# Adding the row term inside PSUM with a three-row bf16 matmul, and keeping the exponentials there

## What is computed

```
el, er = sum(z * attn_l), sum(z * attn_r)
e = leaky_relu(el[src] + er[dst], 0.2)
m = segment_max(e, dst)
ex = exp(e - m[dst])
denom = segment_sum(ex, dst)
out = segment_sum(ex / denom[dst] * z[src], dst) + z
```

## Time and profile before

| what | value |
|---|---|
| time, median of 2 runs | 3789.61 us |
| the two runs | 3783.88 and 3795.34 us |
| span of the profiled execution | 3780.9 us |
| TensorE matmul busy | 2914.6 us (77%) |
| VectorE busy | 1979.8 us (52%) |
| ScalarE busy | 1219.4 us (32%) |

### The profile page before, as it was taken

One profiled execution on the slowest core, in us unless ns is written; L12 is line 12 of the kernel. 1 busy time (PEld: TensorE's weight loads), 2 busy tenths in 40 slices (PEclk: granted clock), 3 DMA queues, 4 the chain that ended last, 5 costly groups with the idle time before them and its releaser, 6 DMA issues.

```text
span 3780.9 us, 46025 instructions
## 1 busy us (share of the span) xinstructions
PE 2914.6 (77%) x14456; PEld 2141.7 (57%) x14457; DVE 1979.8 (52%) x3392; ACT 1219.4 (32%) x1944; POOL 235.8 (6%) x267
## 2 busy tenths in 40 slices
PE   6874999978499996849369269649995994945995
PEld 4542888864288886425257124238884552534773
DVE  6745999945699984551431234556641434233113
ACT  1122778842277774230024101133320222001110
POOL 0000000000000000000001300000000000000112
PEclk9987999989799998979569679869997997965996
DMA  1011121121111212001335621122222100123435
GB/s 61 0 45 46 51 66 55 57 61 34 45 60 54 67 44 62 33 28 29 122 111 196 184 102 60 62 94 78 71 64 96 44 33 20 31 95 110 163 128 168
DMA packets 102475, 276.89 MB, mean 73 GB/s; under 512 B 25358, under 2 KB 38104, under 8 KB 99115
## 3 DMA queue, kind: packets, MB, share of 16 engines
q1 hardware_dynamic: 66794, 194.26, 14.1%
q0 software_dynamic: 32976, 73.59, 7.5%
q10 hardware_dynamic: 2600, 7.68, 0.5%
HBM read 204.99 MB, written 72.91 MB: 74 GB/s over the span
## 4 chain that ended last, share of the span: by engine, by line
PE 42%; DMA 13%; DVE 6%; issue 2%; ACT 1%; SPq 1%; POOL 1%; ACTq 0%; DVEq 0%; POOLq 0%
PE psum L914 16%; PE psum L870 12%; DMA arena<-raw 6%; PE psum L1032 4%; PE psum L1041 4%; PE psum L941 3%; DMA arena<-y_rows,arena 2%; PE psum L931 2%; DVE arena L1460 1%; DMA arena<-r_rows 1%; DMA arena<-xn_rows,arena 1%; PE psum L860 1%; DMA arena<-x 1%; DVE arena L1488 1%; DMA arena<-el_rows 1%
## 5 line engine op out<-in xcount | busy, mean ns | idle before, releaser
L914 PE MATMUL psum<-arena 125*125 125x256 f32 (+3 forms) x2400 | 626.1, 421 | 84.6 <-DVE arena L1490 84.6
L870 PE MATMUL psum<-arena 128*125 128x384 f32 (+1 forms) x1840 | 663.2, 520 | 0.0
L941 PEld LDWEIGHTS psum<-arena 125*125 125x125 f32 x4800 | 580.3, 191 | 71.7 <-DVE arena L1485 16.7
L914 PEld LDWEIGHTS psum<-arena 125*125 125x125 f32 x2400 | 449.5, 189 | 256.3 <-issue 66.9
L941 PE MATMUL psum<-arena 125*125 (+1 forms) x4800 | 568.3, 271 | 16.7 <-DVE arena L1485 16.6
L870 PEld LDWEIGHTS psum<-arena 128*125 128x125 f32 x1840 | 347.6, 191 | 291.2 <-issue 121.9
L1460 DVE CUSTOM_DVE_ANT_0 arena<-arena,no_edge_bias 125x1250 bf16<-125x1250 f32 x300 | 436.5, 1455 | 79.7 <-DMA arena<-el_rows 73.1
L931 PE MATMUL psum<-arena,spread 126*125 126x313 f32 (+1 forms) x1344 | 437.7, 449 | 33.4 <-DMA arena<-r_rows 18.7
L1485 DVE SCALAR_TENSOR_TENSOR arena<-arena,edge_counts 125x625 f32<-125x625 f32 x480 | 381.9, 805 | 79.5 <-ACT arena L1200 79.3
L1187 ACT ACTIVATE arena<-arena,el 125x625 f32<-125x625 f32 x480 | 386.4, 806 | 38.4 <-DMA arena<-el_rows 38.4
L1200 ACT ACTIVATE arena<-psum,el 125x625 f32<-125x625 f32 x336 | 262.6, 782 | 200.9 <-PE psum L931 179.2
(11 more groups left out here) (192 smaller groups left out, 2631.8 us busy)
## 6 DMA issues: line engine op xcount, KB each, us to landing
arena<-el_rows SPq DMA_DIRECT2D x54, 610.4 KB
arena<-in_L_ffn_W SPq DMA_DIRECT2D x16, 1152.0 KB, 9.1
y_rows<-arena SPq DMA_DIRECT2D x47, 384.0 KB, 2.4
arena<-raw SPq DMA_DIRECT2D x40, 375.0 KB
arena<-r_rows SPq DMA_DIRECT2D x24, 610.4 KB
arena<-in_L_w SPq DMA_DIRECT2D x16, 768.0 KB, 6.2
arena<-in_L_gnn_W SPq DMA_DIRECT2D x4, 3072.0 KB, 12.7
z_heads<-arena POOLq DMA_DIRECT2D x10, 1000.0 KB, 12.3
```

Of the source, the lines that this page charges most:

```text
L870: ins = e.matmul(bank[0:P, 0:w], L.xt[u][:, k, :], L.w_sb[:, k, at:at + w], start=(k == 0), stop=(k == L.KT - 1))
L914: ins = e.matmul(banks[2 + 2 * (j % 2) + c][0:P, 0:w], Ph[half][:, s, d * P:(d + 1) * P], (L.zh[u] if L.spill else L.z)[:, s, at:at + w], ...
L941: ins = e.matmul(banks[2 + half][0:P, d * 65:(d + 1) * 65], Ph[half][:, s, d * P:(d + 1) * P], L.z[:, s, h, :], start=(s == 0), stop=(s == ...
```

## The change

The VectorE additions go, and with them `ADD_AT`, the broadcast copies `rb2`, the matrix `spread` and the slots of `r2` and `L.ex`. The block now stays in its pair of PSUM banks from the first stage to the last:

1. `relu` writes straight to `block_exponents(j)` in PSUM. There are two such places, so relu of j may start only when weights of j - 2 are done, and it waits for that on `p_ready`. It is issued after exponentials of j - 2 (before: j - 3).
2. TensorE adds the row for all 20 blocks, in place: a matmul by `ones3` (three rows of ones, bf16) over three partitions that hold r cut into three bf16 parts, with `start=False`.
3. `exponentials` reads and writes the same place in PSUM.
4. `weights` reads it from PSUM.

`max_end`, which now also cuts r into three parts, has ten small VectorE instructions where it had five; the DRAM round trip carries three bf16 rows and takes one load where there were seven. Four matmuls per layer write banks 4 to 7 once before the first block (`primed`).

```
+            if L.batched:
+                    q = r_part[:, u * 3 * T:(u + 1) * 3 * T].rearrange("p (j t) -> p j t", j=3)
+                    st.add(e.scalar_tensor_tensor(out=v[0], in0=er, scalar=SLOPE, in1=v[1], op0=ALU.mult, op1=ALU.subtract))
+                    st.wait()
+                    st.add(e.tensor_copy(r_bf[:, 0:T], v[0]))
+                    st.wait()
+                    st.add(e.tensor_copy(q[:, 0, :], r_bf[:, 0:T]))
+                    st.add(e.tensor_tensor(v[1], v[0], r_bf[:, 0:T], ALU.subtract))
+                    st.wait()
+                    st.add(e.tensor_copy(r_bf[:, T:2 * T], v[1]))
+                    st.wait()
+                    st.add(e.tensor_copy(q[:, 1, :], r_bf[:, T:2 * T]))
+                    e.tensor_tensor(q[:, 2, :], v[1], r_bf[:, T:2 * T], ALU.subtract).then_inc(L.r_ready, 1)
...
-            def lay_r2(h, u, i, first, more):
+            def lay_r3(h, u, i):
                 e.wait_ge(L.rt_sb, L.since["rt_sb"] + h + 1)
                 apart(e)
+                e.dma_start(r3_rows[h, :, :], L.rt3[u]).then_inc(L.r_out[u], 16)
                 e.wait_ge(L.r_out[u], L.since["r_out"][u] + 16 * (i + 1))
                 apart(e)
                 if not isinstance(i, int) or i > 0:
+                    e.wait_ge(L.t_ready, L.since["t_ready"] + 2 * T * (h - 1))
                     apart(e)
+                e.dma_start(L.r3[u], r3_rows[h, :, :].rearrange("(j t) p -> j (t p)", j=3)).then_inc(L.r3_in[u], 16)
...
-                e.wait_ge(L.e_ready, L.since["e_ready"] + 2 * T * h + j + 1)
                 o = block_exponents(j)
                 for at, to in ((0, CUT), (CUT, HALF)):
-                    ins = e.matmul(o[:, at:to], spread[:, :], L.r2[half][:, s % 3, at:to], start=True, stop=True)
+                    ins = e.matmul(o[:, at:to], ones3[:, :], L.r3[u][:, half * HALF + at:half * HALF + to],
+                                   start=False, stop=True, skip_group_check=True)
                 ins.then_inc(L.t_ready, 1)
...
+                e.wait_ge(L.p_ready, L.since["p_ready"] + 2 * T * h + j + 3)
                 apart(e)
-                e.activation(L.r2[half][0:P, s % 3, :], L.erb[u][:, half * HALF:(half + 1) * HALF], ACT.Relu,
+                e.activation(block_exponents(j), L.erb[u][:, half * HALF:(half + 1) * HALF], ACT.Relu,
                              bias=L.el8[:, s, bass.ds(h, 1)], scale=1.0 - SLOPE).then_inc(L.relued, 1)
...
+                e.wait_ge(L.t_ready, L.since["t_ready"] + 2 * T * h + j + 1)
                 apart(e)
-                e.activation(L.ex[j % 4], src, ACT.Exp, bias=L.el2[:, s, bass.ds(h, 1)]).then_inc(L.e_ready, 1)
+                e.activation(block_exponents(j), block_exponents(j), ACT.Exp, bias=L.el2[:, s, bass.ds(h, 1)]).then_inc(L.e_ready, 1)
...
-                    if j + 3 < 2 * T:
-                        relu(h, u, i, j + 3)
+                    if j + 2 < 2 * T:
+                        relu(h, u, i, j + 2)
...
-                    e.scalar_tensor_tensor(out=Ph[half][:, s, :], in0=L.ex[j % 4], scalar=2.0, in1=counts,
+                    e.scalar_tensor_tensor(out=Ph[half][:, s, :], in0=block_exponents(j), scalar=2.0, in1=counts,
                                            op0=ALU.min, op1=ALU.mult).then_inc(L.p_ready, 1)
```

More of the change, by code:

```diff
@@ L38 @@
 BAL_EPS = 0.01
-ADD_AT = [3, 7, 9]
-ADDS, TURNS = 2 * len(ADD_AT), 2 * (T - len(ADD_AT))
-def of_vector(j):
-    return sum(v % T in ADD_AT for v in range(j))
 def split(total, parts):
@@ L253, in graph_transformer @@
         r_rows = dram("r_rows", (12, 2 * T, P))
+        r3_rows = dram("r3_rows", (12, 3 * T, P), BF16)
         z_heads = dram("z_heads", (4, N, 512))
@@ L342, in graph_transformer @@
                 at += 2 * N
-                L.r2 = [carve(at + half * 3 * HALF, P + 1, 3 * HALF).rearrange("p (u d) -> p u d", u=3) for half in range(2)]
-                at += 6 * HALF
+                L.r3 = [carve(at + u * HALF, 3, HALF).bitcast(BF16) for u in range(2)]
+                at += 2 * HALF
                 L.ex = [carve(at + u * HALF, P, HALF) for u in range(4)]
@@ L348, in graph_transformer @@
                 at += 4 * HALF
-                L.rb2 = [carve(at + u * N, P, N) for u in range(2)]
-                at += 2 * N
+                L.rt3 = [carve(at + u * 63, 3 * T, 63).bitcast(BF16)[:, 0:P] for u in range(2)]
+                at += 126
             else:
@@ L536, in lay_r2 @@
                 if not isinstance(i, int) or i > 0:
-                    e.wait_ge(L.added, L.since["added"] + ADDS * (h - 1))
+                    e.wait_ge(L.t_ready, L.since["t_ready"] + 2 * T * (h - 1))
                     apart(e)
-                e.dma_start(L.rb2[u], over(r_rows[h, T:2 * T, :].rearrange("t p -> (t p)"))).then_inc(L.rb2_in[u], 16)
-                for half in range(2):
-                    if not first:
-                        e.wait_ge(L.t_ready, L.since["t_ready"] + TURNS * (h - 1) + TURNS // 2 * (half + 1))
-                        apart(e)
-                    for v in range(3):
-                        e.dma_start(L.r2[half][P:P + 1, v, :],
-                                    r_rows[h, T + half * HT:T + (half + 1) * HT, :].rearrange("(o t) p -> o (t p)", o=1)
-                                    ).then_inc(L.r2_in[half], 16)
-                    if half == 0 and more:
-                        load_el(h + 2, u)
+                e.dma_start(L.r3[u], r3_rows[h, :, :].rearrange("(j t) p -> j (t p)", j=3)).then_inc(L.r3_in[u], 16)
             def move_r(h, u, i):
@@ L577, in rows_of @@
                     load_er(h, u)
-                    lay_r2(h, u, i, False, more)
+                    lay_r3(h, u, i)
+                    if more:
+                        load_el(h + 2, u)
                 with e.Fori(1, L.H // 2 - 1) as i:
@@ L945, in sum_tile, with batched_head @@
                     e.matmul(banks[1][0:1, 0:1], ident[:, 0:1], ident[:, 0:1], start=True, stop=True).then_inc(L.p_free, 1)
-            def batched_head(h, u, first, last):
+            def batched_head(h, u, i, first, last):
                 for j in range(2 * T):
                     half, s = j // T, j % T
-                    if s not in ADD_AT:
-                        exponents(h, j)
+                    exponents(h, u, i, j)
                     if not (first and half == 0):
@@ L955, in batched_head @@
                         turn_r(h + 1, 1 - u)
+            if L.batched:
+                for b in range(4, 8):
+                    ins = e.matmul(banks[b][0:P, 0:512], noti[:, :], MB[:, 0, 0:512], start=True, stop=True)
+                ins.then_inc(L.primed, 1)
             turn_r(0, 0)
             if L.batched:
-                batched_head(0, 0, True, False)
-                batched_head(1, 1, False, False)
+                batched_head(0, 0, 0, True, False)
+                batched_head(1, 1, 0, False, False)
                 with e.Fori(1, L.H // 2 - 1) as i:
                     for u in range(2):
-                        batched_head(2 * i + u, u, False, False)
-                batched_head(L.H - 2, 0, False, False)
-                batched_head(L.H - 1, 1, False, True)
+                        batched_head(2 * i + u, u, i, False, False)
+                batched_head(L.H - 2, 0, L.H // 2 - 1, False, False)
+                batched_head(L.H - 1, 1, L.H // 2 - 1, False, True)
                 for d in range(HT):
@@ L1313, in graph_vector @@
         def graph_vector(e, st):
[L1314 removed]
+            e.wait_ge(gs["in"], 16 * 5)
             st.add(e.memset(zero, 0.0))
+            st.add(e.memset(ones3[:, :], 1.0))
             for w in range(2):
@@ L1528, in finish @@
                     ins.then_inc(L.out_done, 1)
-            def add_r2(h, u, i, j):
-                half, s = j // T, j % T
-                if j == ADD_AT[0]:
-                    e.wait_ge(L.rb2_in[u], L.since["rb2_in"][u] + 16 * (i + 1))
-                e.wait_ge(L.relued, L.since["relued"] + 2 * T * h + j + 1)
-                e.wait_ge(L.p_ready, L.since["p_ready"] + 2 * T * h + j + 1)
-                apart(e)
-                e.tensor_tensor(L.ex[j % 4], L.r2[half][0:P, s % 3, :], L.rb2[u][:, half * HALF:(half + 1) * HALF], ALU.add).then_inc(L.added, 1)
             def batched_head(h, u, i, first, more):
```

59 lines of the change are left out of this document (27 added, 32 removed).

## The result

The changed kernel takes 4312.47 us (two runs, 4310.36 and 4314.57). The kernel before takes 3789.61. The ratio is 1.1376, interval 1.1339 to 1.1413: slower by 13.8%. The forecast of 4101 us had the sign, but the time is 122 us over the upper end of the range.

The account below looks back on a forecast made before the run. TensorE bounded the kernel before, VectorE close behind; a ring of two would bound the changed one. Span 3780.9 + 325.7 - 14 = 4092.6, with 8.7 added 4101 us, 8.2% more; range 4045 to 4190.

Parts of the forecast that it names:

- The ring: In-layer wait on two PSUM places: one turn of three handoffs, 2.43 or 2.57 us a block, 620.0 us a layer.
- The start: Before each layer's first exponentials: one load for seven, first exponentials near 351.5, 7 us earlier, 14 for both layers.
- PSUM: ScalarE and VectorE using PSUM for SBUF: no cost by trace, 0.05 us either way per activation; skill's 65 ns rejected.
- The clock, and what a block costs TensorE at the low clock: TensorE in both layers: clock near 1.0, about 1.5 us a block; at 1.2 GHz 2.76, over the turn.
- Rival A: TensorE's clock falls in the layers: 120 us more if held low, 4221 us, or 4161 in alternation; chance 0.12.
- The price at half clock: TensorE's block at 1.2 GHz: message sum 2.20 plus row matmul 0.56, 2.76 us.
- The drain ... is the same message sums as before: After each layer's last weights: the same message sums as before, so no term in the forecast.

Follow-up runs that it names:

- e4: Kernel before without VectorE's additions, all rows by the old float32 matmul, relu of j waiting for weights of j - 2: 4096.27 us, ratio 1.0798.
- e5: Changed kernel with r and ones in float32, the ones padded with zeros to 125 rows: 4083.11 us, ratio 1.0791.
- e2: Changed kernel with exponentials written to four SBUF slots again, relu of j waiting for exponentials of j - 2: 4300.07 us, ratio 1.1335.
- e6: Changed kernel with the bf16 row of ones padded with zeros to 125 rows, nothing else: 4105.42 us, ratio 1.0849.
- e3: Changed kernel with r and ones in float32, still three rows: 5080.82 us, ratio 1.3393.
- e10: Changed kernel with exponentials in SBUF slots, ones padded to 125 rows, two unread extra matmuls behind every message sum: 4483.64 us, ratio 1.183.
- e12: Changed kernel, exponentials in SBUF, ones padded to 125 rows, unread matmuls per block: four in heads 0 and 1, then two: 3737.25 us, ratio 0.9857.
- e1: Changed kernel with four unread extra bf16 matmuls behind every message sum: 4534.21 and 4698.30 us, too far apart for a ratio.
- e9: Changed kernel with exponentials in SBUF slots and ones padded to 125 rows, no extra matmuls: 4088.81 us, ratio 1.0788.
- e11: Changed kernel with exponentials in SBUF slots, ones padded to 125 rows, three unread extra matmuls behind every message sum: 3818.34 us, ratio 1.0067.
- e13: Changed kernel, exponentials in SBUF, ones padded to 125 rows, unread matmuls per block: four in heads 0 and 1, then one: 4160.80 us, ratio 1.0972.

## Why the prediction was wrong

**The ring: right.** Predicted 2.43 and 2.57 us a turn and 620.0 us a layer. The changed kernel shows 2.48 where TensorE isn't in the way, and e4, which has the ring and of the rest of the change only that the additions are gone, 620.9 us. Its total of 4096 us is 5 under the forecast, and e5's 4083 us are 18 under it. That the totals come so near is in part luck, since both kernels differ from the changed one in other ways.

**The start: right in its terms, with luck in the last digit.** Predicted 351.5 for the first exponentials, measured 351.79. From the turning of r (`turn_r`) to the first exponentials it is 351.79 - 345.91 = 5.88 us, where it was 358.38 - 344.88 = 13.50. But when r is turned differs from kernel to kernel: e2, with the same start, turns it at 350.02 and has its first exponentials at 355.94. The 7 us were to come in both layers; the table shows them once (-6.7), and the stretch between the layers at 5.1 - 10.1 = -5.0 without the drain.

**PSUM: right in the sum.** VectorE's weights from PSUM take 809 ns against 805, not 65 more. Even the 4 ns aren't PSUM's: e2 reads SBUF and has 809 too. These are e2's weights and exponentials in the groups by line:

```profile
L1489 DVE SCALAR_TENSOR_TENSOR arena<-arena,edge_counts 125x625 f32<-125x625 f32 x480 | 388.5, 809 | 646.1 <-ACT arena L1189 646.1
...
L1189 ACT ACTIVATE arena<-psum,el 125x625 f32<-125x625 f32 x480 | 374.9, 781 | 606.6 <-PE psum L917 606.5
```

ScalarE is faster when it writes PSUM: the relu takes 786 ns against 0.80 to 0.82 us, the exponentials 754 against 781 (e2). The two together are about 60 ns of a turn at most, inside the 0.05 allowed for each.

**The clock, and what a block costs TensorE at the low clock: wrong, and this is the step that failed.** The forecast had the ring set the pace, with TensorE's clock "near 1.0" and its work under the turn. The runs showed a clock of 0.50 and 3.00 us a block on TensorE, over the ring's mean of 2.59. It took both, the low clock and the low height: e6 has the ring and the same low clock with full height, and its 4105 us are 4 over the forecast. Rival A had the first half of it with 0.12, and three of its statements fell.

- "In the 5 us before, with 2.42 us of work in them (48%), the clock was 1.00; in the new turn it works about 60%." I took one stretch of 5 us with the clock up as evidence that such a share holds it. That stretch was float32 work over 126 rows, with the clock up already. Two more windows of the kernel before, on either side of those of the earlier trace rows:

```profile
355.00:360.00 5.00, 3.96 (x11) 2.43 (x10) 0.74 (x2) 2.91 (x4) 0.00 (x0) 0.75 0.21 87
...
390.00:400.00 10.00, 10.00 (x73) 8.89 (x72) 10.00 (x15) 7.43 (x11) 0.00 (x0) 1.00 0.29 118
```

  Both kernels come to the layer at 0.50. In the one before the clock rises in the first row matmuls, falls again at about 372 us and is back for good before 390 us. In the changed one TensorE has 2.99 us of work in the 10 us from 350 to 360, all at 0.50, and the clock never rises, at 100% busy from 380 us on either. So neither the share nor the clock at the start was the thing to go by: the work that TensorE was left with is another (bf16, three rows), and e3 and e5 show that its kind matters.
- "At 1.2 GHz ... TensorE would work without pause, as it does in mid-layer, where the clock is 0.98." The first half is so, 100% busy. The conclusion that this would bring the clock back was the mistake: it stayed at 0.50 to the end of the layer. The Trainium skill (TensorE: Matmul & The Clock Gate, "What's actually happening") says that the clock is gated by how busy TensorE has been recently. The trace doesn't agree, if busy is what the profile shows: e10 and e12 have the same 100% at 0.50 and at 1.00, and in e1 600 us of 100% went by at 0.50 before it rose.
- "0.26 x 460 = 120 more, 4221 us". The rival's price was 120 us. The layers took 716.1 - 620.0 = 96.1 us more each, 192 in all, and the drains 20. With these 212 the forecast of 4101 becomes 4313, the time measured.

**The price at half clock.** I had 2.20 + 0.56 = 2.76 us. With full height it is 2.52 (e6), less than that and under the ring's mean. The 0.48 above it is the three-row matmul that holds up the weight loads behind it. The prediction had put the row pair at "0.28 to 0.37" by its columns and called TensorE's cost off the path. It had weighed no cost for the height, though the step from 126 rows to 3 was in the diff.

**How the 523 us come about.** The terms don't simply add up: in each block what ends last decides. The ring gives 4096 at nearly full clock (e4). Half clock at full height gives 4089 without the ring (e9) and 4105 with it (e6). Half clock with three rows gives 4300 without the ring (e2) and 4312 with it. Of the 523 us some 300 are thus lost twice over, by the ring and by the clock, and 207 more come from the height at half clock (4312.5 - 4105.4). Of the experiments only e11 and e12 have neither the ring nor the half clock (nor three rows): they stand 0.7% over and 1.4% under the time before.

**"The drain ... is the same message sums as before": wrong by 20 us**, since it too runs at half clock, 21.07 against 10.99 us.

**What stays open.** What the chip wants to see before it raises the clock. Shown is that the profile's busy share isn't it, that what went before matters (e10, e12), that in float32 full height raises it and three rows don't (e5, e3), and that in bf16 full height alone isn't enough (e6, e9). Two of these pairs, e10 with e12 and e3 with e5, ran on different chips. The kernel before takes the same time on all four chips of the experiments, within 0.2% (3785.03 to 3792.03 us), but that one chip doesn't raise its clock more easily than another wasn't tried. On one and the same chip are e10 with e11, e12 with e13, and e5 with e6. Why e1 fell at about 467 us and rose at about 1071 us stays open; the pause before the fall is a hint only. Nor was it tried how few fillers at the start are enough in e12.

## What to carry to other kernels

When a change takes work off TensorE, the work that is left can run at the half clock and cost more than the work that went: look at the granted clock from the first microseconds of the stage on, and don't take a full busy share as a sign that the clock will be up. A matmul over a few rows between matmuls of full height costs what its columns don't show, and filling up its weights with zeros can win that back. A buffer kept from the first stage of a pipeline to the last makes a ring whose turn is the sum of the handoffs. Count its places before you save the copy.

## What the runs showed of the hardware

- TensorE can be 100% busy in the profile at 1.2 GHz for nearly a whole layer (380 to 1067 us in the changed kernel). Two programs that are equal from head 2 of each layer on ran it at 0.50 and 1.00 (e10, e12).
- The clock can rise after 600 us of 100% busy at 0.50, with no change in the work (e1, at about 1071 us).
- In these kernels a pair of matmuls over 3 rows is followed by 0.42 us (1.2 GHz) in which the loads of 125-row weights stand still, 195 us over the program; with 125 rows there is none.
- Useless matmuls can pay: in e12 two for each block, 0.44 us, and four at the start make the kernel 16.6% faster than with two throughout (3737 against 4484 us).
- Reading PSUM in place of SBUF costs VectorE's 625-column instruction nothing (809 ns in the changed kernel and in e2). Writing PSUM in place of SBUF makes ScalarE's 20 to 27 ns shorter (relu 786 against 806 in the kernel before, exponentials 754 against 781 in e2).
